# Twelve steps of a final stream placed between the last layer's products, and a stream one step shorter

## The reference

```python
x = emb[call]
for l in range(2):                                  # B=2, S=1024, D=192, 12 heads, FF=768
    a = _longformer_attn(x, ...)
    x = _ln(x + a, g1[l], beta1[l])
    h = relu(x @ W1[l].T + b1[l]) @ W2[l].T + b2[l]
    x = _ln(x + h, g2[l], beta2[l])
h = _ln(x, gf, betaf) @ Wc.T + bc                   # 192 -> 128
y = layernorm(norm(h)) ; y = scan(y) @ W_out + conv5(y) ; x = norm(h) + y
h = h + x + gelu(layernorm(x) @ W1 + b1) @ W2 + b2
scores = softmax(norm(h) @ Wg + bg)                 # 8 experts, the best one is taken
h = h + expert_mlp[idx](norm(h)) * score
```

## Time and profile before

| what | us |
|---|---|
| median of 3 runs (lowest to highest) | 917.97 (917.25 to 919.37) |
| the profiled execution, own time | 919.02 |
| its span in the trace | 916.9 |
| PE busy over the span | 809.2 (88%) |
| DVE busy | 634.4 (69%) |
| ACT busy | 563.3 (61%) |
| POOL busy | 567.2 (62%) |

### The profile page before, as it was taken

How to read it: one execution, slowest core, us unless ns; L and a number is a source line. 1 busy time by engine, 2 the same in 40 slices (tenths; PEclk the granted TensorE clock), 3 DMA queues, 4 the chain that set the end, 5 groups by cost and what they waited for, 6 DMA issues and landing times.

```text
span 916.9 us, 23665 instructions
## 1 busy us (share of the span) xinstructions
PE 809.2 (88%) x8467; PEld 617.3 (67%) x8467; DVE 634.4 (69%) x1959; ACT 563.3 (61%) x1559; POOL 567.2 (62%) x820
## 2 busy tenths in 40 slices
PE   5979998999999989989999899999998986887397
PEld 2757766576777666667776666677766664876397
DVE  2769975547899655578997553689975436988454
ACT  2858885437788853267888543778885423565164
POOL 3638885545388856475888554438885546759345
PEclk8989998999999999999999999999999996997599
DMA  2310000142000012430000024200000245001331
GB/s 65 105 47 3 4 13 11 58 139 77 6 4 3 13 35 87 114 92 26 3 3 14 11 81 116 79 5 4 3 3 2 79 121 205 1 3 41 93 103 39
DMA packets 38595, 43.84 MB, mean 48 GB/s; under 512 B 7162, under 2 KB 33881, under 8 KB 38345
## 3 DMA queue, kind: packets, MB, share of 16 engines
q1 hardware_dynamic: 18348, 19.40, 7.1%
q10 hardware_dynamic: 17860, 18.19, 6.7%
q0 software_dynamic: 2272, 4.74, 1.7%
HBM read 20.70 MB, written 21.59 MB: 46 GB/s over the span
## 4 chain that ended last, share of the span: by engine, by line
PE 59%; DVE 21%; issue 5%; SPq 4%; POOL 4%; ACT 4%; DMA 3%; POOLq 0%; DVEq 0%; ACTq 0%
PE bank L1369 7%; DVE p L1011 6%; DVE nmx L1002 5%; PE bank L1575 5%; PE bank L1457 5%; PE bank L1576 5%; PE bank L1506 4%; PE bank L1530 4%; PE bank L1395 3%; PE bank L1406 3%; PE bank L1460 2%; PE bank L1509 2%; PE bank L1680 2%; PE bank L1601 2%; PE bank L1689 2%
## 5 line engine op out<-in xcount | busy, mean ns | idle before, releaser
L573 POOL TENSOR_TENSOR p<-p 128x384 f16<-128x384 f32 (+1 forms) x320 | 283.8, 907 | 103.4 <-ACT p L746 98.7
L1002 DVE TENSOR_REDUCE nmx<-bank 128x1 f32<-128x384 f32 (+1 forms) x384 | 190.6, 511 | 20.7 <-PE bank L1460 16.2
L744 ACT ACTIVATE p<-bank 128x384 f32<-128x384 f32 (+1 forms) x384 | 170.9, 452 | 54.3 <-PE bank L1509 38.0
L1506 PE MATMUL bank<-stack 103*128 103x128 bf16 x1056 | 145.1, 222 | 5.6 <-DMA stack<-mtr 5.1
L746 ACT ACTIVATE p<-bank 128x384 f16<-128x384 f32 (+1 forms) x320 | 144.3, 451 | 0.0
L1509 PE MATMUL bank<-bandb,idb 128*128 128x128 bf16 x672 | 135.3, 222 | 0.0
L1530 PE MATMUL bank<-vst,p 128*128 128x49 bf16 x2112 | 115.8, 185 | 15.2 <-DVE p L1011 13.6
L1457 PE MATMUL bank<-stack 100*128 100x384 bf16 (+1 forms) x384 | 121.2, 316 | 7.3 <-DVE nmx L1002 2.9
L1530 PEld LDWEIGHTS bank<-vst,p 128*128 128x128 f16 x2112 | 89.5, 97 | 32.4 <-DVE p L1011 19.1
L1506 PEld LDWEIGHTS bank<-stack 103*128 103x128 bf16 x1056 | 88.3, 98 | 29.7 <-issue 14.5
L1460 PE MATMUL bank<-bandb,idb 128*128 128x128 bf16 x672 | 101.2, 220 | 0.0
(11 more groups left out here) (253 smaller groups left out, 1818.0 us busy)
## 6 DMA issues: line engine op xcount, KB each, us to landing
xs<-zrow ACTq DMA_DIRECT2D x8, 2193.0 KB, 13.5
xt<-xs SPq DMA_DIRECT2D x23, 129.0 KB, 2.1
w2s<-in_w SPq DMA_DIRECT2D x4, 576.0 KB
mwbs<-in_mwb SPq DMA_DIRECT2D x1, 2064.0 KB, 8.5
mw2s<-in_mw SPq DMA_DIRECT2D x1, 2048.0 KB, 12.8
lnrow<-in_lnr SPq DMA_DIRECT2D x4, 480.0 KB
stack<-mtr SPq DMA_DIRECT2D x96, 3.0 KB
w1b<-in_w SPq DMA_DIRECT2D x4, 291.0 KB
```

The source lines that it names most:

```text
L573: nc.gpsimd.tensor_tensor(p2[:, u % RING, 0:w], p32[:, u % RING, 0:w], p1[:, u % RING, 0:w], ALU.subtract).then_inc(p2_pool, 1)
L744: ins = nc.scalar.activation(p32[:, s % RING, 0:w], ps[2 + s % 3][:, 0:w], ACT.Exp)
L1002: nc.vector.tensor_reduce(nmx[:, vn % 3, h:h + 1], nat_bank(v)[:, 0:w], AX.X, ALU.max, negate=True).then_inc(max_done, 1)
L1506: ins = mm(ps[2 + s % 3][:, blk(i)], stack[0:K_ALL, H + h, blk(m)], stack[0:K_ALL, h, blk(n)], start=True, stop=m == n)
```

## The change

`DEPTH` goes from 13 to 12, so the stream has 28 steps. Stage by stage: z0, its transposes, `wca` and `kept` stay at block t-1; everything behind them works one block later per step (t-3 becomes t-2, t-4 becomes t-3, and so on). Steps 0 to 11 (`FILLED`) are no longer behind the rounds. The bodies of the stream become functions (`stream` on DVE and POOL, `stream_head` and `stream_rest` on PE and ACT), and the list of the last round gets `("head", t)` before and `("rest", t)` after the pair that `STREAM` names. On DVE and POOL a step is done whole at its head. The products y 8 to y 15 of the last round use two banks in place of four (`y_bank`), so that y(i) waits for z(i-2); the stream uses banks 2 to 7 there, with logits in bank 0 and ranks in bank 1 afterwards. The transposed z0 goes to `ata` and `atb` in place of `xa` and `xb`, which still feed the hidden products. The order of SBUF tiles changes, and some first steps wait for the round's last use of a bank.

```diff
-DEPTH = 13
+DEPTH = 12
+FILLED = 12
...
+        def y_bank(i, last):
+            return ps[i % 2 if last and i >= NB else i % 4][:, 0:D]
...
@@ PE, y_block
-                    pe.wait_ge(z_ready, at(z_ready, i - 3))
-                y = ps[i % 4][:, 0:D]
+                    pe.wait_ge(z_ready, at(z_ready, i - 1 if last and i >= NB + 2 else i - 3))
+                y = y_bank(i, last)
...
@@ DVE, statistics of h0, now in stream(t)
-                    i = t - 3
+                    i = t - 2
                     if 0 <= i < NN:
                         dve.wait_ge(kept, i + 1)
                         s_link = ch.mark(nc.vector.bn_stats(sums[:, 1, :], h0[:, i, :]))
...
@@ PE, in stream_rest(t)
+                i = t - 1
+                if 0 <= i < NN:
+                    pe.wait_ge(a0_done, i + 1)
+                    if i:
+                        pe.wait_ge(kept, i)
...
+                    mm(ps[2][:, 0:DM], ata[:, blk(i % NB)], wca[:, :], start=True, stop=False)
...
@@ PE, in the list of a round
+                        if kind == "head":
+                            stream_head(i)
+                        if kind == "rest":
+                            stream_rest(i)
...
@@ every engine, behind the rounds
-            for t in range(NN + DEPTH):
+            for t in range(FILLED, NN + DEPTH):
+                stream_head(t)
+                stream_rest(t)
...
+STREAM = {("y", 9): (0,), ("y", 10): (1,), ("y", 11): (2,), ("hid", 6): (3,), ("hid", 7): (4,), ("hid", 8): (5,),
+          ("hid", 9): (6,), ("hid", 10): (7,), ("hid", 11): (8,), ("y", 12): (9,), ("y", 13): (10,), ("y", 14): (11,)}
...
 def seq_c(rnd):
 
+    if rnd == B * L - 1:
+        seq = []
+        for kind, i in _seq_c():
+            if kind == "tr" and i >= NB:
+                continue
+            steps = STREAM.get((kind, i), ())
+            seq += [("head", t) for t in steps]
+            seq.append((kind, i))
+            seq += [("rest", t) for t in steps]
+        return seq
```

More of the change, by code:

```diff
@@ L222, in program @@
         rs = sb("rs", [P, 2, 5], F32)
+        mw2s = sb("mw2s", [P, E, EH // P, DM], F32)
+        mwbs = sb("mwbs", [P, E, WB], F32)
+        tiles = sb("tiles", [P, 5, E], F32)
+        tmp = sb("tmp", [P, NT * E], F32)
+        tmp2 = sb("tmp2", [P, NT * E], F32)
+        more = sb("more", [P, E], F32)
+        tof = sb("tof", [P, 5, NT], F32)
+        toi = sb("toi", [P, 3, NT], I32)
         xt = sb("xt", [P, XBUF, RW], F32)
@@ L623, in _ @@
             sent = 0
-            for t in range(NN + DEPTH):
[L625 to L638, removed]
+            for t in range(FILLED, NN + DEPTH):
+                stream(t)
                 placed = max([0] + [e for (_, e), c in zip(GROUPS, CHOSEN) if t >= c + 2])
@@ L684, in first_pieces, with stream_head, stream_rest @@
                                      ACT.Copy).then_inc(qk_hi, 1)
+            def stream_head(t):
+                if t == 0:
+                    nc.scalar.activation(gs[0:1, 0, 0:1], lfa[0:1, 0:1], ACT.Gelu)
+                i = t - 1
+                if 0 <= i < NN:
+                    act.wait_ge(t0_mm, i + 1)
+                    nc.scalar.activation(ata[:, blk(i % NB)], ps[4][0:DLO, 0:P], ACT.Identity, bias=lfa[:, 1:2],
+                                         scale=lfa[:, 0:1])
+                    nc.scalar.activation(atb[0:DHI, blk(i % NB)], ps[4][0:DHI, P:2 * P], ACT.Identity, bias=lfb[0:DHI, 1:2],
+                                         scale=lfb[0:DHI, 0:1]).then_inc(a0_done, 1)
+                i = t - 8
+                if 0 <= i < NN:
+                    act.wait_ge(m1_mm, i + 1)
+                    for m in range(2):
+                        ins = nc.scalar.activation(gl[:, i % 2, m, :], ps[6][:, blk(m)], ACT.Gelu, bias=ab1s[:, m:m + 1])
+                    ins.then_inc(gelu_done, 1)
+                i = t - 3
+                if 0 <= i < NN:
+                    b, n = divmod(i, NB)
+                    act.wait_ge(t1_mm, i + 1)
+                    nc.scalar.activation(xn[:, b, 2 + n * P:2 + (n + 1) * P], ps[5][:, 0:P], ACT.Identity, bias=l12[:, 1:2],
+                                         scale=l12[:, 0:1]).then_inc(a1_done, 1)
+            def stream_rest(t):
+                i = t - 1
+                if 0 <= i < NN:
+                    act.wait_ge(hw_mm, i + 1)
+                    nc.scalar.activation(h0[:, i, :], ps[2][:, 0:DM], ACT.Copy).then_inc(kept, 1)
+                i = t - 7
+                if 0 <= i < NN:
+                    act.wait_ge(t2_mm, i + 1)
+                    nc.scalar.activation(ht[:, i % 2, :], ps[4][:, 0:P], ACT.Identity, bias=l12[:, 3:4],
+                                         scale=l12[:, 2:3]).then_inc(a2_done, 1)
+                i = t - 11
+                if 0 <= i < NN:
+                    act.wait_ge(t3_mm, i + 1)
+                    nc.scalar.activation(xm[:, i % 2, :], ps[5][:, 0:P], ACT.Copy).then_inc(a3_done, 1)
             for k in range(2 * NC):
@@ L811, in _ @@
                             nc.scalar.activation(hid[:, m, :], ps[6 + i % 2][:, :], ACT.Relu).then_inc(h_relu, 1)
+                        if kind == "head":
+                            stream_head(i)
+                        if kind == "rest":
+                            stream_rest(i)
+                        if kind == "hid":
                             if rnd == 0 and i == FF // P:
@@ L1090, in _ @@
                             normed(i, y, zt[:, i % 4, :]).then_inc(z_ready, 1)
+                        if kind == "head":
+                            stream(i)
             nc.vector.memset(tiles[:, 3, :], 1.0)
```

342 lines of the change are left out of this document (180 added, 162 removed).

## The result

The change took 937.32 us (median of 4 runs, 935.0 to 939.14), the kernel before 917.61 beside it (914.34 to 919.37). The ratio is 1.0218, 95% interval 1.0181 to 1.0255: slower by 19.7 us, against 12 predicted. The profiled execution took 935.0 us, its span is 933.2.

A forecast was written before the change was run, and what follows sets the result against it. A closed PE-ACT-DVE ring was taken to bound the interleaved steps: +8.4 us up to the first choice of experts, plus 3.5 for the low clock, gave +11.9 on 919.02, so 930.9, or 929.9 us as median; range 920 to 939.

The forecast's parts named there:

- a ring: Each stream step: transposes, product, wca, kept, statistics of h0, z0, next transposes; 2.79 us from wca on with scan.
- the part: From the start of product y8 to the first choice of experts; predicted 8.4 us longer before the clock's term.
- The ring's size: Waits and ring passes from y8 to the first choice of experts: +8.4 us, 6.5 of it by T(12).
- y8 to T(1): From product y8's start to T(1), T(t) being the start of stream step t's z0 transposes; T(1) predicted at 735.5 us.
- the six steps with a hidden product: T(3) to T(9): ring passes of 4.95 us twice, 5.06 three times and 5.51 once, together 30.6 us.
- the last three with y: T(9) to T(12): DVE must take y before the next step; 7.65, 8.13 and 12.85 us, together 28.6.
- Behind T(12): Steps 12 to 16: ring without a product, 4.38 us a step against 3.97; 1.9 us new, everything later at nothing.
- The clock: PE's waits lower its granted clock: 3.5 us taken, two to three short slow stretches, between ends 0 and 11.7.
- rival B: Clock stays low through the first steps: 8.4 + 11.7 = +20.1 us, 938 us; chance 0.16.
- Rival C: PE's own work binds, not the ring: -19.5 us, 898.5; wins if mean ring T(1) to T(12) falls under 5.4; chance 0.12.
- Two banks at nothing: Two-bank rule for y8 to y15: met before DVE's own waits, so costs nothing while DVE is late.
- 0.2% is what can be told apart: Whole kernel: 0.2% (1.8 us) taken as the smallest difference told apart from no change.

The follow-up runs named there:

- e1: The change with 29 stream steps again, so DVE reads h0 two steps after PE's wca product, steps 0 to 11 still between the products: 924.75 us, ratio 1.0063.
- e6: The change (28 steps) with DVE and GpSimd taking each of y8 to y13 behind the step interleaved with it, not ahead: 926.86 us, ratio 1.0097.
- e3: The change with added products that nobody reads, run in PE's waits up to step 11: 929.92 us, ratio 1.0121.
- e5: e1 (29 steps) with DVE and GpSimd taking each of y8 to y13 behind the step interleaved with it: 912.80 us, ratio 0.9921.
- e7: e5 with two more stream steps inside, around y15 and ahead of its taking: 900.97 us, ratio 0.9808.
- e2: The change with nothing interleaved: all 28 steps behind the last product, two banks for y8 to y15: 940.04 us, ratio 1.0226.

## Why the prediction was right, and where it was not

**The direction and the mechanism: right.** PE, ACT and DVE form a ring when the statistics of h0 come in the next step, and y8 to y15 lie in a second one through DVE's order. e1 and e6 open one each, and each takes 14 to 15 us from the part.

**The ring's size: right, each term to 0.6 us and their sum to 0.1.** e3 is the change at full clock up to step 11, so it can be held against the terms of the sum. y8 to T(1) 7.83 (8.1 predicted), then 5.84 (5.7) and 6.82 (6.5); the six steps with a hidden product 30.06 (30.6); the last three with y 7.48, 8.29 and 13.28 (7.65, 8.13, 12.85); y8 to T(12) 79.60 us, 79.5 predicted. Behind T(12) 4.43 or 4.44 a step (4.38). In the change itself the hidden steps at full clock take 5.00, 5.00, 5.00 and 5.44.

**Behind T(12), the first step: missed by 1.6 to 1.9 us.** T(12) to T(13) takes 6.32 us in e3 at a mean clock of 0.56 and 5.94 in the change at 0.72, for 4.38. The range of the clock's term counted it (2.3 for two passes), the forecast did not by name. What I put at nothing there held: the longest weight load takes 13.3 us to land, and the time behind the first choice is 98.4 us for 99.1.

**The clock: the step that failed.** I took 3.5 us, "two to three short stretches like that of rows 7", from the ends 0 and 11.7. It cost all of the upper end: the part is 20.06 us longer, of which the ring's own terms are 8.4, so 11.7 are left; measured, 9.4 are what e3 gives back, and 1.9 stay in T(12) to T(13). The mechanism was right, the price was that of rival B (+20.1, 938), to 0.1 us in the part and 0.7 in the time. That it agrees so closely is partly luck. My 11.7 was 4.0 for y10 and y11, 3.4 for two hidden products, 2 for small ones around them and 2.3 behind T(12). Measured, e3 gives back 3.6 us from T(1) to T(3), 3.4 from T(3) to T(9) and 2.9 from T(11) to T(12), where I had no term.

What my choice overlooked, as I now read the rows (no run tests this reading by itself): in a ring PE cannot make up for the slow clock. A y product at 1.2 GHz takes 4.05 us instead of 2.12 and DVE gets it later, but the wait of PE behind it stays long (3.02 and 3.58 us after 3.69), because it is made of DVE's links. So the waits came again and again, and slow time was 34 us and not the 7 to 10 I assumed. A closed ring alone does not do it: that of e6 has waits for z0 of 0.54 to 2.52 us up to T(11), and the clock stays at 1.00. The rule of the Trainium skill that I set beside rival B (page "TensorE: Matmul & The Clock Gate", section "A second HAM failure mode: psum-queue depth-cycling", short idles between groups of products that make the clock swing) spoke for B, and 0.16 was too little for it. The trace of the change agrees with it, since the clock fell and came back several times, in or behind waits for z0 of 1.24 to 3.69 us; that of e6 shows that waits of up to 2.52 us can also leave the clock alone.

**Rival C, faster if the ring is open: its condition fits, its size was not reached.** It would begin to win at a mean ring under 5.4 us from T(1) to T(12). e5 has (783.18 - 728.63) / 11 = 4.96 and is faster than before, e6 with (800.87 - 731.88) / 11 = 6.3 is not; no kernel lies close to 5.4. Its -19.5 needed PE's work alone to bound. Opening both rings gives -8.4 in the part, since DVE's order around y14 and y15 still holds PE (T(11) to T(12) takes 13.27 us in e5), and e7 gives -13.5. There PE is busy for all of T(9) to T(12); what is left against C is about the twenty-ninth step (4.0 us) and T(13) to T(14), 6.47 us for 3.97.

**Two banks at nothing: right in this place, for a reason that I gave only in passing.** In e2, with the products close together, the rule costs 7.9 us. Between the steps DVE frees each bank before PE comes back, but for y15, which waits 1.03 us; I had counted that one in the 12.85. Once y is taken later the rule costs again: in e5 and e6 three and four of the y products wait 0.89 to 1.14 us for a bank.

**"0.2% is what can be told apart": too fine.** The runs of the kernel before lie between 911.1 and 923.3 us, and with ten runs of a kernel the interval of a ratio was still 0.6% wide.

## What to carry to other kernels

Before work of one regime is put between the steps of another, write down each step's chain of releases from engine to engine until it closes; what lies between two of its links is added to every step, however much room the busy shares show. A shorter pipeline distance is paid in nearly every step (here 0.46 us in full steps and 1.9 to 2.2 in the first three, against 4 us saved once), so the distance and the placement should be tried apart. When a tuned engine has to wait inside a ring, price the low clock at its upper end, and ask first whether the consumer can take the product one step later: with 29 steps and y taken later the same interleaving won 0.8%, and 1.9% with two steps more.

## What the runs showed of the hardware

In e6 the granted clock stayed at 1.00 through 59 us in which PE was busy 10.36 of 16.40, 25.01 of 32.10 and 9.09 of 10.70 us, with waits for z0 of 0.54 to 2.52 us. In the change it fell in a wait of 3.69 us, and PE was busy 9.19 of the 13.70 us in which it was 0.50 throughout, which begin in a wait of 3.02 us and hold one of 3.58. I had not expected that six takings of y, moved by one place in DVE's order, would end the slow stretches up to T(11). But the wait just before does not tell it all: in e7 the clock fell behind a wait of 1.61 us at T(4), and its mean was 0.91 over 19.50 us in which PE was busy for 19.49. And the same products ahead of y8 took between 723.96 and 729.83 us in the profiled executions of the change and of e1 to e7, so a difference of two medians of less than about 5 us says less here than the length of the edited part.
